# A third state of a selective scan is multiplied by C on TensorE, and the output copy keeps one buffer

## The chip, the cores and the metric

The kernel runs on one core of one Trainium2 chip. The time is device microseconds of one execution of the whole program, and a version's time is the median of its runs. The engines are named as the profile names them: PE is TensorE (its matmuls), PEld its weight loads, DVE is VectorE, ACT is ScalarE, POOL is GpSimd, and SP is SyncE, which here only issues DMAs.

## What is computed

The program is one layer of a metaformer on an input of 1024 channels and 64 x 64 pixels. A first part normalises and runs a decaying sum over channels. The second part is a bidirectional selective scan over the 4096 pixels as a sequence, and it takes most of the time:

```python
def step(h, inp):
    u_t, dt_t, B_t, C_t = inp
    dA = jnp.exp(dt_t[:, :, None] * A)
    h = dA * h + (dt_t * u_t)[:, :, None] * B_t[:, None, :]
    y = jnp.einsum('bdn,bn->bd', h, C_t)
    return (h, y)
...
y = (y_fwd + y_bwd) * jax.nn.silu(z.transpose(0, 2, 1))
out = y @ out_proj_w.T
```

There are 2048 inner channels d and 16 states n for each of them, and two directions. What the change touches is the second line of the recurrence's output: every state h[d, n, t] is multiplied by C[t, n] and the 16 products are summed.

## The kernel before

**Units.** `stage_scan` cuts the sequence into 8 chunks of T = 512 pixels and the inner channels into DB = 16 blocks of 128. One direction and chunk and block is a unit. There are 256: units 0 to 127 go backward, 128 to 255 forward. A chunk is 16 units in a row; below, the chunks are numbered 0 to 15. The code of each engine is written out unit by unit, and in a unit step by step for the states n = 0 to 15. Nothing reorders it: each engine runs its own list and waits on semaphores.

**One state on the engines.** In step n, ACT makes da = exp(delta * A[n]) into one of two PSUM banks (`da`, L1094), after it has saved the last column of the state of step n-2 (`save`, L1074); that save waits until scan n-2 is done. DVE runs the recurrence as one scan instruction (L1239), from `da`, the carried `state` and `w` = du * B, which POOL makes four states at a time (`weigh_b`, L1192). The result must then be multiplied by C and turned (pixels to partitions), and all 16 are summed in the PSUM bank `yT`. There are three ways for the product:

- states in VN (0, 1, 3, 6, 7, 9, 12 to 15): the scan writes PSUM (`h`), DVE multiplies by the broadcast C (`weigh`, L1249, into `hc`), and PE adds the transpose of `hc` into `yT` (L973, four 128x128 pieces);
- states in PN (2, 5, 8, 11): the scan writes SBUF (`hs`), POOL multiplies two states at once (`weigh_c`, L1202, into `hp`), and PE adds the transpose (L934);
- states in TN (4, 10): the scan writes SBUF, PE turns the state itself (`turn`, L868) into the bank `in_ps`, ACT copies it to `h_turned` (`turn_copy`, L1051), and PE multiplies it by a diagonal matrix of C (`add_turned`, L877) into `yT`. The diagonals `c_diag` are made by ACT (L1066) in the first unit of every chunk from the columns `c_col`, which SP loads as single elements (`load_c_columns`, L721).

DVE's multiplies don't stand behind each scan but in groups, behind the scans of 2, 5, 8, 11, 13 and 15.

**What else runs through the units.** PE works one chunk ahead: in backward units it projects x (`in_step`, L846, halves at steps 0 and 2, into `in_ps`), ACT copies it out at step 7 (L1025), PE runs the convolution as four diagonal matmuls into the bank `dt_ps` (`conv_step`, L853, step 5), and ACT copies that at step 10 (L1028). In forward units PE projects z for the unit itself, and the convolutions are for the chunk ahead. The last 16 backward units (chunk 7) project nothing and have an order of their own for the convolution (`TURN`: convolution at step 2, copy at 7). The bank `dt_ps` also takes the projection to dt (L841), which ACT reads at step 1 (`dt_read`, L994), in a chunk's last unit at step 4. ACT then makes `delta` for the next unit in the steps up to 6 (L999 to L1018).

**The output.** `yT_copy(b - 1)` (L1044) stands in ACT's step 2 of unit b and copies `yT` into one of two buffers `y_out`; SP stores it (L769). Ahead of the copy ACT waits for

```python
if b >= 1:
    act.wait_ge(S["stored"], stored_to(b - 1))
...
nc.scalar.activation(y_out[:, b % 2], yT[:], ACT.Copy).then_inc(S["yT_copied"], 1)
```

where `stored_to(b)` counts every store (yT, x, xc, z) that SP issues up to and with its unit b. SP waits in the same order: its unit b issues the stores of yT, xc and z, in a chunk's last unit also eight broadcasts of B and C (L713, 1 MB each) and the c columns between them, and at its end waits for `stored_to(b)` before it loads what the next units need.

## Time and profile before

| | |
|---|---|
| median of 3 runs | 8235.12 us (8234.53 to 8238.75) |
| the profiled execution | 8231.93 us, span 8230.1 us |
| the 256 units, from the first scan to the last | 728.4 to 7180.0 us |
| DVE busy, whole span | 7156.1 us (87%) |
| POOL busy | 6715.8 us (82%) |
| PE busy | 7136.7 us (87%) |
| ACT busy | 5349.8 us (65%) |
| granted TensorE clock, mean of the span | 0.959 |

The busy shares are of the whole span, with the stages ahead of and behind the scan. In a timeline the first column is the start in us from the span's start and the second the duration; instructions that follow one another are merged with their count. Two neighbours overlap by some 0.1 us at their ends, so what an instruction costs its engine is the distance to the next start, not its own duration. TensorE splits each float32 matmul of real data in two (8 in the trace for 4 in the code), and a transpose not. Steps below are given as "+x", in us after the start of the unit's first scan.

### The profile page before, as it was taken

What the parts mean: (1) busy time and instruction counts of PE and PEld (TensorE: products, weight loads), DVE (VectorE), ACT (ScalarE), POOL (GpSimd) and SP (SyncE); (2) the same over time, 40 slices, a digit from 0 to 9 for tenths busy, and PEclk for the clock granted to TensorE, in tenths of its full rate; (3) what the DMA queues carried; (4) which work ended last, traced back from release to release, by engine and by line L of the source; (5) the groups of instructions that cost most, each with busy time, mean ns of one, the idle gap of its engine ahead of it and who ended that gap; (6) DMA issues with size and microseconds to landing.
All of it is one profiled execution on the core that took longest, in us unless ns stands there. A gap on an engine that the chain in (4) does not pass through costs nothing. (4 is left out here: it accounts for less than half of the span.)

```text
span 8230.1 us, 114768 instructions
## 1 busy us (share of the span) xinstructions
PE 7136.7 (87%) x32512; PEld 4393.1 (53%) x32512; DVE 7156.1 (87%) x7788; ACT 5349.8 (65%) x12640; POOL 6715.8 (82%) x2320
## 2 busy tenths in 40 slices
PE   6578888888888888877899999999999988789999
PEld 3344555555555555554555555555555555534444
DVE  6913999999999999999999999999999999934443
ACT  6634777777777777777777777777777777610000
POOL 5513999999999999999999999999999999821110
PEclk8789999999999999998999999999999999889999
DMA  3363232323232323221323232323233332153442
GB/s 103 90 191 128 70 118 66 118 70 118 67 118 68 119 67 118 68 98 44 113 79 128 76 128 77 131 79 126 89 116 104 104 107 70 63 191 133 136 140 76
DMA packets 557719, 844.05 MB, mean 103 GB/s; under 512 B 129472, under 2 KB 276928, under 8 KB 539712
## 3 DMA queue, kind: packets, MB, share of 16 engines
q1 hardware_dynamic: 557120, 837.10, 31.1%
q8 instruction: 250, 4.10, 0.2%
q14 instruction: 349, 2.86, 0.1%
HBM read 583.89 MB, written 253.02 MB: 102 GB/s over the span
## 5 line engine op out<-in xcount | busy, mean ns | idle before, releaser
L1192 POOL TENSOR_TENSOR scan_w<-scan_du,scan_bcast_b 128x2048 f32<-128x2048 f32 x1023 | 4623.9, 4544 | 45.0 <-DVE scan_h L1239 6.6
L1239 DVE TENSOR_TENSOR_SCAN scan_h<-scan_da,scan_state,scan_w 128x512 f32<-128x512 f32 x2560 | 3185.3, 1276 | 44.2 <-ACT scan_da L1094 27.7
L1094 ACT ACTIVATE scan_da<-scan_delta,scan_prm 128x512 f32<-128x512 f32 x4096 | 2803.1, 685 | 0.0
L973 PE MATMUL scan_yT<-all_ident,scan_hc 128*128 128x128 f32 x10240 | 1540.1, 281 | 660.4 <-DVE scan_hc L1249 659.6
L1239 DVE TENSOR_TENSOR_SCAN scan_hs<-scan_da,scan_state,scan_w 128x512 f32<-128x512 f32 x1536 | 1891.9, 1258 | 45.2 <-ACT scan_da L1094 44.7
L973 PEld LDWEIGHTS scan_yT<-all_ident,scan_hc 128*128 128x128 f32 x10240 | 1175.3, 143 | 1395.5 <-DVE scan_hc L1249 1047.1
L846 PE MATMUL scan_in_ps<-scan_hn,scan_win 128*128 128x512 f32 x3840 | 1732.3, 594 | 13.6 <-issue 13.6
L1249 DVE TENSOR_TENSOR scan_hc<-scan_h,scan_bcast_c 128x512 f32<-128x512 f32 x2560 | 1637.3, 671 | 2.1 <-ACT scan_state L1074 0.7
L1202 POOL TENSOR_TENSOR scan_hp<-scan_hs,scan_bcast_c 128x1024 f32<-128x1024 f32 x512 | 1209.3, 2362 | 49.9 <-DVE scan_hs L1239 42.9
L846 PEld LDWEIGHTS scan_in_ps<-scan_hn,scan_win 128*128 128x128 f32 x3840 | 693.6, 191 | 715.6 <-issue 715.6
L1074 ACT ACTIVATE scan_state<-scan_h 128x1 f32<-128x1 f32 x2560 | 429.5, 168 | 982.8 <-DVE scan_h L1239 977.0
L853 PE MATMUL scan_dt_ps<-scan_x,scan_diag 128*128 128x512 f32 x1920 | 888.5, 606 | 101.2 <-ACT scan_x L1025 101.2
L1398 PE MATMUL out_o_ps<-out_yg,out_wout 128*128 128x512 f32 x2048 | 891.0, 594 | 0.0
L1366 POOL TENSOR_TENSOR out_yf<-out_yf,out_yb 128x512 f32<-128x512 f32 x128 | 162.5, 1270 | 744.7 <-DMA out_z<-z 744.7
L1398 PEld LDWEIGHTS out_o_ps<-out_yg,out_wout 128*128 128x128 f32 x2048 | 385.9, 191 | 464.8 <-issue 464.8
L1376 ACT ACTIVATE out_sz<-out_z 128x512 f32<-128x512 f32 x128 | 80.7, 630 | 826.1 <-DMA out_z<-z 826.1
L853 PEld LDWEIGHTS scan_dt_ps<-scan_x,scan_diag 128*128 128x128 f32 x1920 | 351.4, 193 | 480.9 <-issue 480.9
L877 PE MATMUL scan_yT<-scan_h_turned,scan_c_diag 128*128 128x128 f32 x4096 | 576.6, 287 | 0.0
L934 PE MATMUL scan_yT<-all_ident,scan_hp 128*128 128x128 f32 x4096 | 553.8, 280 | 0.0
L877 PEld LDWEIGHTS scan_yT<-scan_h_turned,scan_c_diag 128*128 128x128 f32 x4096 | 535.4, 204 | 0.5
L1427 DVE COPY out_o<-out_o_ps 128x512 f32<-128x512 f32 x64 | 44.2, 691 | 523.6 <-PE out_o_ps L1398 321.9
L934 PEld LDWEIGHTS scan_yT<-all_ident,scan_hp 128*128 128x128 f32 x4096 | 485.1, 146 | 0.0
(122 smaller groups left out, 6918.3 us busy)
## 6 DMA issues: line engine op xcount, KB each, us to landing
yT<-scan_y_out SPq DMA_DIRECT2D x257, 256.0 KB, 2.0
scan_win<-winx SPq DMA_DIRECT2D x128, 512.0 KB, 3.7
xc<-scan_xc_out SPq DMA_DIRECT2D x256, 256.0 KB, 2.0
scan_xc<-xc SPq DMA_DIRECT2D x256, 256.0 KB, 4.1
scan_bcast_b<-bc SPq DMA_DIRECT2D x64, 1024.0 KB, 8.0
scan_bcast_c<-bc SPq DMA_DIRECT2D x64, 1024.0 KB, 8.2
scan_win<-winz SPq DMA_DIRECT2D x128, 512.0 KB, 4.6
scan_x<-x_pad SPq DMA_DIRECT2D x128, 257.5 KB, 2.6
```

What stands on the lines that cost most here:

```text
L846: last = nc.tensor.matmul(bank, win[:, s, i], hn[:, i], start=(i == 0), stop=(i == KT - 1))
L853: last = nc.tensor.matmul(bank, diag[:, s, i], x[:, s, at:at + T], start=(i == 0), stop=(i == TAPS - 1))
L877: last = nc.tensor.matmul(yT[:, tb], c_diag[:, k, tb], h_turned[:, tb * P:(tb + 1) * P], start=False, stop=False)
L934: last = nc.tensor.matmul(yT[:, tb], hp[:, i, tb * P:(tb + 1) * P], ident[:], is_transpose=True, start=False, stop=False)
L973: last = nc.tensor.matmul(yT[:, tb], hc_slot(b, n)[:, tb * P:(tb + 1) * P], ident[:], is_transpose=True, start=(i == 0 and tb == 0), stop= ...
L1074: nc.scalar.activation(state_of(unit_, n_), h_slot(unit_, n_)[:, col:col + 1], ACT.Copy).then_inc(S["h_saved"], 1)
L1094: nc.scalar.activation(da[:, n % 2], delta[:, s], ACT.Exp, scale=decay(b, n)).then_inc(S["exp_done"], 1)
L1192: nc.gpsimd.tensor_tensor(w[:, g], du[:].unsqueeze(1).to_broadcast([P, G, T]), bcast_b[:, g * G:(g + 1) * G], ALU.mult).then_inc(S["w_done ...
L1202: nc.gpsimd.tensor_tensor(hp[:, i:i + 2], hs[:, HS[first]:HS[first] + 2], bcast_c[:, first:second + 1:second - first], ALU.mult).then_inc( ...
L1239: nc.vector.tensor_tensor_scan(flip(b, h_slot(b, n)), flip(b, da[:, n % 2]), flip(b, w[:, n // G, n % G]), state_of(b, n), ALU.mult, ALU.a ...
L1249: nc.vector.tensor_tensor(hc_slot(b, n), h_slot(b, n), bcast_c[:, n], ALU.mult).then_inc(S["hc_done"], 1)
L1398: last = nc.tensor.matmul(o_ps[:, q % 2], wout[:, q, b], yg[:, g, b], start=(b == 0), stop=(b == DB - 1))
```

## The change

State 1 moves from VN to TN. Its scan writes SBUF, DVE's multiply for it is gone, and PE turns it at step 3 into `dt_ps` (the other turned states still use `in_ps`), ACT copies it at step 7 ahead of the copy of the projection, and PE multiplies it by its diagonal at step 7. `y_out` has one buffer instead of two, so that `yT_copy` waits for the stores of one unit more. `TURN` goes, and chunk 7 uses `NORMAL`. The diagonals are 12 per chunk instead of 8, and start at step 2.

```diff
-TN = [4, 10]
+TN = [1, 4, 10]
...
-        y_out = sc.sb("y_out", [P, 2, TB, P])
+        y_out = sc.sb("y_out", [P, TB, P])
...
-        TURN = dict(diag=1, conv=2, xc=7, proj=8)
...
-            return [(a, TURN if back(b) and not back(a) else NORMAL)] if a < NU else []
+            return [(a, NORMAL)] if a < NU else []
...
-                return dict(mm=(6, 12), copy=(10, NS - 1), add=(12, NS - 1))
-            return dict(mm=(8, 12), copy=(12, NS - 1), add=(12, NS - 1))
+                return dict(mm=(3, 6, 12), copy=(5, 10, NS - 1), add=(5, 12, NS - 1))
+            return dict(mm=(3, 8, 12), copy=(7, 12, NS - 1), add=(7, 12, NS - 1))
+
+        def turn_bank(k):
+            return in_ps if k else dt_ps
...
-        C_DIAG_AT = (3, 3, 8, 8, 9, 9, 11, 11)
+        C_DIAG_AT = (2, 2, 3, 3, 8, 8, 9, 9, 11, 11, 13, 13)
...
                 pe.wait_ge(S["scan_done"], b * NS + TN[k] + 1 + SCR)
-                pe.wait_ge(S["in_copied"], (in_copies(b) if b or k else DB + 1) + 2)
+                if k == 0:
+                    pe.wait_ge(S["dt_read"], min(b + 2, NU))
+                    pe.wait_ge(S["xc_copied"], min(b + DB + 1, NU) + 2 if b else DB + 2)
+                else:
+                    pe.wait_ge(S["in_copied"], (in_copies(b) if b or k > 1 else DB + 1) + 2)
...
             def conv_step(a, b):
                 pe.wait_ge(S["dt_read"], min(b + 2, NU))
+                pe.wait_ge(S["h_turn_copied"], b * NTN + 1)
...
-                if b >= 1:
-                    act.wait_ge(S["stored"], stored_to(b - 1))
+                if b >= 0:
+                    act.wait_ge(S["stored"], stored_to(b))
                 act.wait_ge(S["hc_used"], (b + 1) * NV + NOUT)
-                nc.scalar.activation(y_out[:, b % 2], yT[:], ACT.Copy).then_inc(S["yT_copied"], 1)
+                nc.scalar.activation(y_out[:], yT[:], ACT.Copy).then_inc(S["yT_copied"], 1)
...
+                    if n == turn_steps(b)["copy"][0]:
+                        turn_copy(b, 0)
                     for i, when in in_steps_of(b):
                         if n == when["copy"]:
```

The lists of the engines show three places. The first is PE in an ordinary forward unit, from the first half of the projection on. Before (scan_hc is the product on its way into yT, scan_hs a state that is turned):

```order
L846 MATMUL scan_in_ps<-scan_hn,scan_win 128x512 x4
L973 MATMUL scan_yT<-all_ident,scan_hc 128x128 x8
L846 MATMUL scan_in_ps<-scan_hn,scan_win 128x512 x4
L973 MATMUL scan_yT<-all_ident,scan_hc 128x128 x4
L853 MATMUL scan_dt_ps<-scan_x,scan_diag 128x512 x4
L973 MATMUL scan_yT<-all_ident,scan_hc 128x128 x8
L934 MATMUL scan_yT<-all_ident,scan_hp 128x128 x8
L868 MATMUL scan_in_ps<-all_ident,scan_hs 128x128 x4
```

The same place in the changed kernel (its line numbers are 2 to 9 higher):

```order
L848 MATMUL scan_in_ps<-scan_hn,scan_win 128x512 x4
L980 MATMUL scan_yT<-all_ident,scan_hc 128x128 x4
L848 MATMUL scan_in_ps<-scan_hn,scan_win 128x512 x4
L874 MATMUL scan_dt_ps<-all_ident,scan_hs 128x128 x4
L980 MATMUL scan_yT<-all_ident,scan_hc 128x128 x4
L855 MATMUL scan_dt_ps<-scan_x,scan_diag 128x512 x4
L980 MATMUL scan_yT<-all_ident,scan_hc 128x128 x4
L883 MATMUL scan_yT<-scan_h_turned,scan_c_diag 128x128 x4
L980 MATMUL scan_yT<-all_ident,scan_hc 128x128 x4
L941 MATMUL scan_yT<-all_ident,scan_hp 128x128 x8
L874 MATMUL scan_in_ps<-all_ident,scan_hs 128x128 x4
```

Four transposes ahead of the projection's second half are gone, four stand behind it, and the product with the diagonal stands between the convolution and the next turn.

The second place is ACT in the first unit of a chunk, from its step 2 (scan_da is the exponential, scan_v a link of the chain to delta). Before:

```order
L1094 ACTIVATE scan_da<-scan_delta,scan_prm 128x512
L1044 ACTIVATE scan_y_out<-scan_yT 128x512
L999 ACTIVATE scan_v<-scan_v,scan_prm 128x512
L1074 ACTIVATE scan_state<-scan_h 128x1
L1094 ACTIVATE scan_da<-scan_delta,scan_prm 128x512
L1066 ACTIVATE scan_c_diag<-all_ident,scan_c_col 128x128 x2
L1074 ACTIVATE scan_state<-scan_hs 128x1
```

Changed:

```order
L1101 ACTIVATE scan_da<-scan_delta,scan_prm 128x512
L1073 ACTIVATE scan_c_diag<-all_ident,scan_c_col 128x128 x2
L1051 ACTIVATE scan_y_out<-scan_yT 128x512
L1006 ACTIVATE scan_v<-scan_v,scan_prm 128x512
L1081 ACTIVATE scan_state<-scan_hs 128x1
L1101 ACTIVATE scan_da<-scan_delta,scan_prm 128x512
L1073 ACTIVATE scan_c_diag<-all_ident,scan_c_col 128x128 x2
```

Two diagonals now stand ahead of the copy of yT. At step 7 of every unit the list gains one row ahead of the copy of the projection:

```order
L1101 ACTIVATE scan_da<-scan_delta,scan_prm 128x512
L1058 ACTIVATE scan_h_turned<-scan_dt_ps 128x512
L1032 ACTIVATE scan_z_out<-scan_in_ps 128x512
L1081 ACTIVATE scan_state<-scan_h 128x1
L1101 ACTIVATE scan_da<-scan_delta,scan_prm 128x512
```

The third place is SP in the last unit of a forward chunk, changed; before, the second c_col row had no x2, and nothing else differs:

```order
L715 DMA scan_bcast_c<-bc 128x2048 [waits scan_hc_done,scan_hp_done]
L723 DMA scan_c_col<-bc 128x4x1 [waits scan_c_diag_done]
L723 DMA scan_c_col<-bc 128x4x1 x2
L798 DMA z<-scan_z_out 128x512 [waits n1_transposed]
L691 DMA scan_x<-x_pad 128x515 [waits scan_stored,n1_var_ready]
```

A third column stands ahead of the store of z, and the load of x behind it is the first that waits for `stored`.

## Rows read from the trace of the kernel before

**Rows 1.** DVE's waits, 800 to 7000 us: total, times, longest.

```profile
DVE scan_hs L1239 <- ACT scan_da L1094: 39.2, 67, 1.2
```

**Rows 2.** DVE's timeline in a backward unit (it starts at 2404.32).

```profile
2403.14 1.26 DVE L1249 TENSOR_TENSOR scan_hc<-scan_h,scan_bcast_c 128x512 f32<-128x512 f32 x2
2404.32 2.45 DVE L1239 TENSOR_TENSOR_SCAN scan_h<-scan_da,scan_state,scan_w 128x512 f32<-128x512 f32 x2
...
2415.58 1.26 DVE L1239 TENSOR_TENSOR_SCAN scan_hs<-scan_da,scan_state,scan_w 128x512 f32<-128x512 f32 x1
...
2427.97 0.67 DVE L1249 TENSOR_TENSOR scan_hc<-scan_h,scan_bcast_c 128x512 f32<-128x512 f32 x1
```

**Rows 3.** POOL's timeline over the same unit.

```profile
2397.26 2.36 POOL L1202 TENSOR_TENSOR scan_hp<-scan_hs,scan_bcast_c 128x1024 f32<-128x1024 f32 x1
...
2422.11 2.35 POOL L1202 TENSOR_TENSOR scan_hp<-scan_hs,scan_bcast_c 128x1024 f32<-128x1024 f32 x1
```

**Rows 4.** ACT's timeline in the same unit, steps 5, 7 and 8.

```profile
2410.35 0.17 ACT L1074 ACTIVATE scan_state<-scan_h 128x1 f32<-128x1 f32 x1 [0.83 <-DVE scan_h L1239]
...
2414.28 0.58 ACT L1025 ACTIVATE scan_x<-scan_in_ps 128x512 f32<-128x512 f32 x1
2414.76 0.16 ACT L1074 ACTIVATE scan_state<-scan_h 128x1 f32<-128x1 f32 x1
2414.81 0.68 ACT L1094 ACTIVATE scan_da<-scan_delta,scan_prm 128x512 f32<-128x512 f32 x1
```

**Rows 5.** PE's timeline in a forward unit (it starts at 4444.94).

```profile
4450.61 3.60 PE L846 MATMUL scan_in_ps<-scan_hn,scan_win 128*128 128x512 f32 x8
4454.05 0.60 PE L973 MATMUL scan_yT<-all_ident,scan_hc 128*128 128x128 f32 x4
4454.48 3.60 PE L853 MATMUL scan_dt_ps<-scan_x,scan_diag 128*128 128x512 f32 x8
...
4462.81 0.66 PE L973 MATMUL scan_yT<-all_ident,scan_hc 128*128 128x128 f32 x4 [2.16 <-DVE scan_hc L1249]
4463.30 1.02 PE L858 MATMUL scan_proj_ps<-scan_xc_out,scan_wx 128*96 128x512 f32 x2
```

**Rows 6.** The unit at 4394.7, two units earlier, PE's timeline.

```profile
4412.55 0.67 PE L973 MATMUL scan_yT<-all_ident,scan_hc 128*128 128x128 f32 x4 [2.15 <-DVE scan_hc L1249]
4413.04 1.88 PE L858 MATMUL scan_proj_ps<-scan_xc_out,scan_wx 128*96 128x512 f32 x2
```

**Rows 7.** Windows: length, busy PE PEld DVE ACT POOL, clock, DMA share, GB/s.

```profile
3552.00:3967.00 415.00, 297.78 (x1536) 205.22 (x1535) 400.37 (x417) 299.24 (x745) 393.76 (x129) 0.89 0.20 65
4394.70:4419.60 24.90, 22.74 (x104) 14.01 (x103) 24.90 (x27) 18.76 (x47) 24.51 (x9) 0.93 0.25 79
4444.90:4469.80 24.90, 22.46 (x115) 14.13 (x113) 24.90 (x28) 19.20 (x49) 24.51 (x9) 1.00 0.24 80
```

**Rows 8.** Timeline of ACT and DVE in the unit at 4419.61, step 7 to 8.

```profile
4430.06 0.60 ACT L1025 ACTIVATE scan_z_out<-scan_in_ps 128x512 f32<-128x512 f32 x1 [0.43 <-PE scan_in_ps L846]
...
4431.34 1.28 DVE L1239 TENSOR_TENSOR_SCAN scan_hs<-scan_da,scan_state,scan_w 128x512 f32<-128x512 f32 x1 [0.38 <-ACT scan_da L1094]
```

**Rows 9.** SP's timeline at the end of a forward chunk.

```profile
4358.96 2.65 SPq L721 DMA_DIRECT2D scan_c_col<-bc  x2
4361.72 7.73 SPq L796 DMA_DIRECT2D z<-scan_z_out  x1
4374.77 0.33 SPq L689 DMA_DIRECT2D scan_x<-x_pad  x1
```

**Rows 10.** Line L721, the same two loads: from issue to landing.

```profile
DMA to landing us min/median/max: 12.7/13.6/14.6
```

**Rows 11.** ACT's timeline in the next chunk's first unit (it starts at 4369.02).

```profile
4371.61 0.60 ACT L1044 ACTIVATE scan_y_out<-scan_yT 128x512 f32<-128x512 f32 x1 [0.46 <-PE scan_yT L973]
...
4373.97 0.69 ACT L1066 ACTIVATE scan_c_diag<-all_ident,scan_c_col 128x128 f32<-128x128 f32 x2 [0.51 <-DMA scan_c_col<-bc]
```

**Rows 12.** DVE's timeline in a chunk's last unit (it starts at 4342.72), step 8.

```profile
4355.22 1.28 DVE L1239 TENSOR_TENSOR_SCAN scan_hs<-scan_da,scan_state,scan_w 128x512 f32<-128x512 f32 x1 [1.15 <-ACT scan_da L1094]
```

More of the change, by code:

```diff
@@ L769, in unit @@
                 sp.dma_start(yT_d[direction(b - 1)][(b - 1) % HALF + 1 if b else 0],
-                             y_out[:, (b + 1) % 2]).then_inc(S["stored"], LOAD)
+                             y_out[:]).then_inc(S["stored"], LOAD)
                 if at == DB - 1 and more:
@@ L830, in _ @@
             hold(sp, S["yT_copied"], NU + 1, S["passed"])
-            sp.dma_start(yT_d[0][HALF], y_out[:, 1]).then_inc(S["stored"], LOAD)
+            sp.dma_start(yT_d[0][HALF], y_out[:]).then_inc(S["stored"], LOAD)
             hold(sp, S["stored"], stored_to(NU - 1) + LOAD, S["passed"])
@@ L867, in turn @@
                 for tb in range(TB):
-                    last = nc.tensor.matmul(in_ps[:, tb * P:(tb + 1) * P], h_slot(b, TN[k])[:, tb * P:(tb + 1) * P],
+                    last = nc.tensor.matmul(turn_bank(k)[:, tb * P:(tb + 1) * P], h_slot(b, TN[k])[:, tb * P:(tb + 1) * P],
                                             ident[:], is_transpose=True, start=(tb == 0), stop=(tb == TB - 1))
@@ L903, in in_step @@
                     if b or i > DB:
-                        pe.wait_ge(S["h_turn_copied"], b * NTN if b else 1)
+                        pe.wait_ge(S["h_turn_copied"], b * NTN if b else 2)
                     in_proj(i % 2, 0, KT // 2)
@@ L1050, in turn_copy @@
                     act.wait_ge(S["h_turned_used"], b * NTN + k)
-                nc.scalar.activation(h_turned[:], in_ps[:], ACT.Copy).then_inc(S["h_turn_copied"], 1)
+                nc.scalar.activation(h_turned[:], turn_bank(k)[:], ACT.Copy).then_inc(S["h_turn_copied"], 1)
             def diagonal(s, db):
@@ L1136, in unit @@
                             xc_copy(a % 2, block_of(a))
-                    for k in range(NTN):
+                    for k in range(1, NTN):
                         if n == turn_steps(b)["copy"][k]:
```

## The prediction

> **What bounds the kernel now.** The page's busy shares come first: DVE and POOL are near full in every slice of the scan, PE is close, ACT is far from it. A share doesn't say which wait ends last, so the next view is DVE's waits: between 800 and 7000 us its largest wait is on ACT's exponential ahead of a scan into SBUF, 39.2 us over 67 times, the longest 1.2 [rows 1]. DVE is the bound, with some losses that ACT hands it. The third view is the timelines of one backward unit. The pair of multiplies ahead of the unit returns after 24.83 us [rows 2]; POOL's second pair product returns after 24.85 us [rows 3]. The reader is to see that both engines are full at the same pace. ACT then shows where it is tight: it starts step 5 as soon as scan 3 ends (it waited 0.83 for it), works without a pause, and its exponential of step 8 ends at 2415.49 for a scan that starts at 2415.58 [rows 2, 4]. There is no slack between the end of scan 3 and scan 8.
>
> **The ordinary unit.** Taken away: one DVE multiply. Two of them take from 2403.14 to 2404.32, so one costs 0.59 [rows 2]. It stood behind scan 2, ahead of scan 3, so scan 3 and ACT's step 5 come 0.59 earlier. Added in ACT's step 7: a copy of a PSUM bank, which costs what the copy there costs now, 0.48 to the next start [rows 4]. It lies in the very stretch that has no slack, so scan 8 comes 0.59 - 0.48 = 0.11 earlier, and with the 0.09 between exponential and scan used, 0.16 at best. Behind scan 8 nothing changes. A unit takes 24.72.
>
> Is the turned state there in time? PE loses four transposes ahead of the projection's second half and gains four behind it, 0.43 either way (4454.05 to 4454.48) [rows 5]. So it is ready when the projection was, at 4454.21 or +9.27. ACT asked for the projection at 2414.28, +9.96, and will now ask at +9.37 [rows 2, 4, 5]. The margin is 0.10; I count no wait. What is late next is the convolution, which now waits for that copy: it starts at about +10.0 instead of +9.54 [rows 5], and ends at +13.6. Queued behind it are the products of states 6 and 7; DVE has six buffers for them and doesn't notice. ACT copies the convolution in step 10, not before +14, so that is hidden. The product with the diagonal is 8 matmuls of the trace, 0.87 at the transposes' pace. PE waits 2.16 for the product of state 9 [rows 5]; 2.16 - 0.5 - 0.87 - 0.1 leaves 0.7, so PE has the room.
>
> POOL at 24.85 would be the next bound, but it runs ahead: at 2422.11, when it turns to the pair product, it has finished the four inputs for scans 0 to 3 of the next unit, which begins at 2404.32 + 24.83 = 2429.15 [rows 2, 3]: a lead of 7 us. A lag of 0.13 a unit uses up 1.8 us of that in the 14 ordinary units of a chunk, and the chunk's end gives it back. There are 15 x 14 = 210 ordinary units outside chunk 7: 210 x -0.11 = **-23.1 us**.
>
> **The clock in forward units.** In the forward chunks PE's work stands in one piece and its idle time too. After such a wait of 2.15 us the next two matmuls of the projection to B, C and dt take 1.88 us in one unit and 1.02 in another [rows 5, 6]; the granted clock is 0.93 over that unit and 1.00 over the other [rows 7], so for some microseconds it is the lower of its two levels, 1.2 GHz. The unit after it pays: the copy of z waits 0.43 for PE and scan 8 waits 0.38 [rows 8]. The units start at 4394.68, 4419.61 and 4444.94, so they take 24.93 and 25.33; against 24.83 the pair loses 0.6. It returns in every third unit, 0.2 a unit over the 98 ordinary units of chunks 8 to 14 (chunk 15 has no convolution). After the change the wait is split in two, 0.5 ahead of the convolution and 0.7 behind. I take it that the clock then stays at 2.4 GHz: 98 x -0.2 = **-19.6**. The other end is that the drops stay, and then every third unit also gets the 0.48 on top, since there ACT waits for PE: 0 instead of -19.6, and +0.16 x 98 = 16 more.
>
> The Trainium skill (TensorE: Matmul & The Clock Gate, What's actually happening) says that a throttled clock is the default and that activity releases it. By that rule more PE work in the gaps helps; rows 6 and 7 agree that the drop follows idle time. The sum above stands without it.
>
> **The first unit of a forward chunk.** This is the dear place. SP issues two c columns, then the store of z, whose issue alone takes 7.73 us, then waits for the stores until 4374.77 [rows 9], +5.7 of the next unit. The first column landed at 4358.96 + 12.7 = 4371.7 [rows 9, 10], the second when ACT's diagonal began, 4373.97 [rows 11]: a column costs 2.3. The third makes the columns land at +7.3 and the store behind them at about +8.0. Now ACT's copy of yT stands at +2.59 [rows 11] and waits for older stores only. In the changed kernel it stands behind two diagonals and waits for this store: +8.0. Behind it in ACT's queue is everything that leads to scan 8: copy, link and step 3 take 1.85 (4371.61 to 4373.97 - 0.51), two diagonals 0.6, step 4 two passes of some 0.65, steps 5 to 8 take 5.14 plus the new 0.48 [rows 4, 11], together 9.4. Scan 8 starts at +17.4. Today it is 2.59 + 1.85 + 0.51 + 0.6 + 1.3 + 5.14 = +12.0. That is 5.4 for each of 7 chunk starts (8 to 9 up to 14 to 15; the last has lighter work ahead of it, so one less): **+37**. Bounds: the column costs the store nothing, the copy starts at +5.7, 2.3 less, -16; or each of the three columns pushes the store once more, +16. In other units the same wait is free: a store takes about 2 us and the copy comes half a unit later.
>
> Again the page beside it: the Trainium skill (DMA: Bandwidth & Descriptors, Queues, rings and completion order) says that a DMA's increment lands only after every earlier write of the same DMA engine. By this rule z's completion must wait for the third column, as in my sum; without the rule the time would be 8228. Rows 9 and 10 fit: z was issued behind the second column and counted as landed 0.7 after it.
>
> **The other chunk edges.** A chunk's last unit reads dt late, and scan 8 waits 1.15 for ACT [rows 12], so the copy comes in full: 16 x 0.48 = **+7.7**. In the first unit of a backward chunk (and of chunk 8) the columns are early, there is no z, and ACT gets two diagonals ahead of the yT copy, 0.6, where it now waits 0.46 for PE as in [rows 11], plus 0.48: 8 x 0.6 = **+4.9**. Unit 0 waits for the columns too: **+2**.
>
> **Chunk 7.** 415 us for 16 units are 25.9 a unit, at a clock of 0.89 [rows 7]; DVE loses time because ACT waits in step 7 for the convolution. That copy moves to step 10, which frees step 7. But the convolution moves too, from +4 to +10. At 3.60 [rows 5] it ends at +13.6 and the unit is an ordinary one, -1.2. At the lower clock throughout it takes 7.2, ends at +17.2, and scan 11 (due at +15.4) comes 3.1 late, +1.9. PE idles more before it than today, so I take the middle, 0 for 15 units, with -18 and +28 as ends.
>
> **The sum.** -23.1 - 19.6 + 37 + 7.7 + 4.9 + 2 + 0 = +8.9. On the profiled execution's 8231.93 that is 8240.8; the median is 3.2 above it, so 8244.
>
> **The rivals.**
> - *The clock still drops in every third forward unit.* For it: the wait of 2.16 is followed by a drop in one unit and by none in another [rows 5, 6], so the length of that wait alone doesn't decide. Against it: the wait is what the change shortens, to a third. It decides if PE's longest wait stays near 2 us. 8244 + 19.6 + 16 = 8280, slower. Chance 0.15.
> - *The turned state is late.* ACT asks at +9.37 with a margin of 0.10; 0.2 of wait costs 42: 8286, slower. Chance 0.1.
> - *POOL binds.* If its lead is smaller than I think, units stay at 24.85 and the -23 is lost: 8267. Chance 0.06. Chunk 7 at its slow end gives 8272, chance 0.06.
> - *The store isn't pushed.* 8228, no change. Chance 0.13. With chunk 7 at its fast end too, 8210, faster; chance 0.17.
> - The forecast, gains and losses that cancel: chance 0.33.
>
> **How the numbers follow.** What is less than 0.2% (16.5 us) can't be told from no change here. Faster gathers the last case and some of the store's (0.2), slower the first four rivals less their near edge (0.35), the same holds the rest (0.45). The range leaves out the clock and the late turn at their far ends and what lies under 8210: 8208 to 8282.
>
> **What the next profile would show.** Right: DVE's scan 8 waits about 0.5 for ACT in every unit, the unit takes 24.7 in both directions, the granted clock of forward chunks is 1.00, PE's wait ahead of state 9's product falls to 0.7, and ACT's yT copy waits for a DMA once per forward chunk until +8. Wrong: a new wait of ACT on PE ahead of the turn's copy, a POOL product that DVE waits for, or a clock of 0.97 as before.

## The result and the profile after

The changed kernel takes 8221.5 us (median of 20 runs, 8212.26 to 8232.26), the kernel before 8232.15 in the same comparison (20 runs, 8217.56 to 8238.75). The ratio is 0.9987, 95% interval 0.9981 to 0.9993: a small gain, 10.7 us, where a loss of 8.9 us was forecast. Both values are within 0.2% of no change; the sign was forecast wrong.

The page of the profiled execution (8212.7 us, span 8210.9) has DVE at 7011.3 us (85%), PE at 7300.4 (89%), ACT at 5512.2 (67%), POOL at 6711.8 (82%). DVE does one multiply a unit less, PE and ACT do more. DVE's waits between 800 and 7000 us, total, times, longest (before: [rows 1]; there the scans into PSUM, scan_h, waited 6.4 us over 13 times):

```profile
DVE scan_hs L1248 <- ACT scan_da L1101: 136.7, 247, 3.0
DVE scan_h L1248 <- ACT scan_da L1101: 24.6, 22, 3.1
DVE scan_hs L1248 <- POOL scan_hp L1211: 5.0, 4, 2.2
```

DVE now waits for ACT in nearly every unit instead of in one of four, up to 3 us. In the lines of a timeline the square brackets give the engine's idle time ahead of the instruction and what ended it. The timelines of ACT and then of DVE in a backward unit (its scan 0 starts at 2389.90):

```profile
2399.26 0.58 ACT L1058 ACTIVATE scan_h_turned<-scan_dt_ps 128x512 f32<-128x512 f32 x1
2399.74 0.58 ACT L1032 ACTIVATE scan_x<-scan_in_ps 128x512 f32<-128x512 f32 x1
```
```profile
2400.99 1.28 DVE L1248 TENSOR_TENSOR_SCAN scan_hs<-scan_da,scan_state,scan_w 128x512 f32<-128x512 f32 x1 [0.34 <-ACT scan_da L1101]
```

The new copy stands in step 7, 0.48 from start to start, without a wait ahead of it: the turned state was there in time. That holds for all ordinary units; in the last units of 13 chunks ACT waits 1.13 us for PE's turn, where before it waited for PE's projection (0.59 in the unit at 4342.72). PE's timeline in a forward unit (its scan 0 starts at 4409.4), beside [rows 5]:

```profile
4418.09 0.60 PE L874 MATMUL scan_dt_ps<-all_ident,scan_hs 128*128 128x128 f32 x4
...
4419.47 3.67 PE L855 MATMUL scan_dt_ps<-scan_x,scan_diag 128*128 128x512 f32 x8 [0.34 <-issue]
...
4427.16 0.66 PE L980 MATMUL scan_yT<-all_ident,scan_hc 128*128 128x128 f32 x4 [0.94 <-DVE scan_hc L1258]
```

The wait of 2.16 has become 0.34 and 0.94. Windows over chunk 7, chunks 10 to 14 and chunk 15, columns as in [rows 7]:

```profile
3534.00:3959.00 425.00, 315.82 (x1667) 215.26 (x1666) 390.30 (x401) 310.01 (x767) 393.36 (x129) 0.82 0.20 65
4757.00:6763.00 2006.00, 1857.23 (x9592) 1208.43 (x9591) 1951.17 (x2001) 1597.10 (x3901) 1965.42 (x642) 1.00 0.32 104
6763.00:7163.00 400.00, 319.04 (x1750) 229.47 (x1749) 388.86 (x398) 284.18 (x691) 380.85 (x124) 0.95 0.17 58
```

The clock is 1.00 over whole forward chunks (0.97 before), but 0.82 in chunk 7, where it was 0.89, and chunk 7 is 10 us longer. Last, a forward chunk's first unit, whose scan 0 starts at 4356.64: SP's timeline, then ACT's, beside [rows 9, 11].

```profile
4346.85 9.22 SPq L723 DMA_DIRECT2D scan_c_col<-bc  x3
4356.18 0.46 SPq L798 DMA_DIRECT2D z<-scan_z_out  x1
```
```profile
4361.12 0.69 ACT L1073 ACTIVATE scan_c_diag<-all_ident,scan_c_col 128x128 f32<-128x128 f32 x2 [2.38 <-DMA scan_c_col<-bc]
4361.77 0.60 ACT L1051 ACTIVATE scan_y_out<-scan_yT 128x512 f32<-128x512 f32 x1
```

Issuing z now takes 0.46; the 7.7 us for which SP was held up fall on the third column. ACT waits for the columns to +4.5, then copies yT at +5.1. The forecast had +8.0.

**Where the time went.** The start of scan 0 of each unit in both traces gives the periods; their differences, after minus before, sum to the terms of the prediction (mean periods in brackets):

| term | forecast | measured, us |
|---|---|---|
| ordinary backward units, chunks 0 to 6 (97; 24.85 to 24.70) | -10.7 | -14.0 |
| ordinary units of chunks 8 to 14 (98; mean 25.05 to 24.70) | -30.4 | -33.9 |
| first units, forward chunks (7; 25.7 to 28.5; chunk 15 24.8 to 27.2) | +37 | +18.8 |
| first units, backward chunks and chunk 8 (7) | +4.2 | +2.3 |
| last units outside chunk 7 (14) | +6.7 | +7.1 |
| chunk 7 (415.3 to 424.9) | 0 | +9.6 |
| chunk 15 behind its first unit | -1.5 | +2.3 |
| units 0 and 1 | +2 | -1.9 |
| scan stage (the forecast has 1.6 more in chunk 7 and the very last unit) | +7.3 | -9.6 |

The two profiled executions differ by 19.2 us, the medians by 10.7. The scan stage's 9.6 is the change's; 7.0 of the rest lie ahead of the scans, in code that is the same: the first scan started anywhere between 721.3 and 734.4 us in the profiles of this study. So the experiments are read by the same decomposition, beside their ratio. Each is one profiled execution, and terms that an edit doesn't touch differ too: units 0 and 1 by up to 4.5 us in sum, the 14 last units by up to 4, chunk 7 by 1.

### The profile page after: what moved, and what is told of

It is laid out like the page before. It is cut to its first block and busy times, and to the rows that moved or that the text cites. A ratio compares the mean times of both kernels' runs of the same rounds, so it can differ in the third digit from the quotient of the medians.

```text
span 8210.9 us, 119471 instructions
## 1 busy us (share of the span) xinstructions
PE 7300.4 (89%) x34560; PEld 4560.6 (56%) x34560; DVE 7011.3 (85%) x7532; ACT 5512.2 (67%) x12960; POOL 6711.8 (82%) x2320
## 5 line engine op out<-in xcount | busy, mean ns | idle before, releaser
L1248 DVE TENSOR_TENSOR_SCAN scan_h<-scan_da,scan_state,scan_w 128x512 f32<-128x512 f32 x2304 | 2883.9, 1278 | 68.6 <-ACT scan_da L1101 52.3
L1248 DVE TENSOR_TENSOR_SCAN scan_hs<-scan_da,scan_state,scan_w 128x512 f32<-128x512 f32 x1792 | 2198.9, 1260 | 145.2 <-ACT scan_da L1101 140.1
L980 PE MATMUL scan_yT<-all_ident,scan_hc 128*128 128x128 f32 x9216 | 1443.9, 280 | 437.4 <-DVE scan_hc L1258 431.6
L980 PEld LDWEIGHTS scan_yT<-all_ident,scan_hc 128*128 128x128 f32 x9216 | 1066.0, 142 | 1016.6 <-DVE scan_hc L1258 678.4
L1258 DVE TENSOR_TENSOR scan_hc<-scan_h,scan_bcast_c 128x512 f32<-128x512 f32 x2304 | 1479.8, 669 | 0.5
L855 PE MATMUL scan_dt_ps<-scan_x,scan_diag 128*128 128x512 f32 x1920 | 926.6, 627 | 153.9 <-ACT scan_x L1032 101.1
L1081 ACT ACTIVATE scan_state<-scan_h 128x1 f32<-128x1 f32 x2304 | 386.9, 168 | 693.0 <-DVE scan_h L1248 692.3
L883 PE MATMUL scan_yT<-scan_h_turned,scan_c_diag 128*128 128x128 f32 x6144 | 819.2, 277 | 0.0
L883 PEld LDWEIGHTS scan_yT<-scan_h_turned,scan_c_diag 128*128 128x128 f32 x6144 | 753.2, 193 | 0.8 <-issue 0.5
L1081 ACT ACTIVATE scan_state<-scan_hs 128x1 f32<-128x1 f32 x1792 | 352.9, 197 | 237.1 <-DVE scan_hs L1248 236.0
```

Of the source, the lines that this page charges most:

```text
L855: last = nc.tensor.matmul(bank, diag[:, s, i], x[:, s, at:at + T], start=(i == 0), stop=(i == TAPS - 1))
L883: last = nc.tensor.matmul(yT[:, tb], c_diag[:, k, tb], h_turned[:, tb * P:(tb + 1) * P], start=False, stop=False)
L980: last = nc.tensor.matmul(yT[:, tb], hc_slot(b, n)[:, tb * P:(tb + 1) * P], ident[:], is_transpose=True, start=(i == 0 and tb == 0), stop= ...
L1081: nc.scalar.activation(state_of(unit_, n_), h_slot(unit_, n_)[:, col:col + 1], ACT.Copy).then_inc(S["h_saved"], 1)
L1248: nc.vector.tensor_tensor_scan(flip(b, h_slot(b, n)), flip(b, da[:, n % 2]), flip(b, w[:, n // G, n % G]), state_of(b, n), ALU.mult, ALU.a ...
L1258: nc.vector.tensor_tensor(hc_slot(b, n), h_slot(b, n), bcast_c[:, n], ALU.mult).then_inc(S["hc_done"], 1)
```

## The experiments

Ratios are to the kernel before in the same comparison, with the 95% interval. "Scan stage" is the sum of periods against that of the kernel before's profile, -9.6 for the change as given.

**The first unit of a forward chunk.** Three kernels take the two waits of ACT's copy apart.

```diff
-  act.wait_ge(S["stored"], stored_to(b))              # in yT_copy
+  act.wait_ge(S["y_stored"], (b + 1) * LOAD)          # own count; SP's yT store increments it
```

> The changed kernel, but ACT's copy of yT waits only for the store of yT before it, which gets a count of its own, and no longer for the store of z. The profile of the changed kernel has the copy at +5.1 us of the first unit of a forward chunk; the wait listed there is the diagonal's, ahead of the copy, for the c columns (gap 2.4 us, to +4.5), and z's store lands at +5.1. Theory A, the record's (the copy waits for z): the copy returns to +2.6, first forward units fall from 28.1 to about 25.7 us, 6 to 7 of them: 8205 us, ratio to before 0.997. Theory B (two waits end within 0.6 us, and the diagonals in front of the copy hold it alone): nothing moves, 8221 us, ratio 0.9987.

Measured: 8221.31, 0.9990 (0.9981 to 0.9999), scan stage -9.7. First forward units stay 2.7 us over before on average, as in the changed kernel. That is theory B's forecast.

```diff
-  C_DIAG_AT = (2, 2, 3, 3, 8, 8, 9, 9, 11, 11, 13, 13)
+  C_DIAG_AT = (3, 3, 4, 4, 8, 8, 9, 9, 11, 11, 13, 13)
```

> The changed kernel, but the diagonals of state 1 are built in ACT's steps 3 and 4 instead of 2 and 3, so behind the copy of yT. Theory C (the c columns alone hold the copy, the wait for z is empty): the copy returns to +2.6 and first forward units to about 25.7 us, 8205 us. Theory B (both waits end at about +5): the copy stays at +5.0, now for z's store, and the time stays within 3 us of 8221.

Measured: 8228.11, 0.9993 (0.9984 to 1.0002), scan stage -3.1. Now the same ACT copy names the other wait (timeline, unit at 4369.1):

```profile
4375.49 0.60 ACT L1051 ACTIVATE scan_y_out<-scan_yT 128x512 f32<-128x512 f32 x1 [4.26 <-DMA z<-scan_z_out]
```

So the wait is theory B's. The time isn't: it was to stay within 3 us of 8221, and the first forward units cost 26.0 us in sum instead of 18.8. Part of it is that two more diagonals (0.6 us) now come behind the wait instead of between the two; z also landed 0.3 us later on average in this profile.

> The changed kernel with both: the store of yT on a count of its own and the diagonals of state 1 in steps 3 and 4. All theories: the copy of yT at +2.6. Theory B expects that only this one of the three gains: first forward units 26.1 us (25.65 to 25.83 before, less 0.59 of multiply, plus 0.48 of copy and 0.6 of two more diagonals), so 2 to 3 us for each of 7: 8205 us, ratio 0.997. Theories A and C expect no more here than from the one part that each names.

Measured: 8208.06, 0.9971 (0.9962 to 0.9981), scan stage -20.6. The copy is at +2.0; first forward units cost 6.0 us in sum over before instead of 18.8. Taking away either wait alone gains nothing, taking away both gains 13 us. Two of these units still take 27.5 to 27.7 us, against 25.8 to 26.2 in the others. In them the columns' landing holds the diagonals in step 3 for 0.8 to 0.9, the granted clock is 0.94 instead of 1.00, and the convolution takes 5.37 us instead of 3.67, so that scan 11 waits 0.96 for ACT. PE's timeline in the unit at 4369.12:

```profile
4381.05 5.37 PE L856 MATMUL scan_dt_ps<-scan_x,scan_diag 128*128 128x512 f32 x8 [1.26 <-issue]
```

The changed kernel has two such units (29.4 and 29.1 us, clock 0.94), so a part of its +18.8 comes by way of a longer convolution and not directly of a wait for a DMA.

**What a column costs.** Two parts of the change are put alone into the kernel before.

```diff
-  c_col = sc.sb("c_col", [P, NTN, TB])
+  c_col = sc.sb("c_col", [P, NTN + 1, TB])     # and a load of state 1's column behind the two
```

> The kernel before, with one edit: SP also loads the c column of state 1, which nobody uses (the diagonals wait for all three). The record's step: a column costs 2.3 us of DMA time at a chunk's start, so the last one lands at +7.3 of a forward chunk's first unit (+4.95 before) and the diagonals start then: 2.3 us for each of 8 chunk starts, 8247. Theory from the profile of after (all that was issued by then lands when the broadcasts' backlog is through, and the third column only takes over the 7.6 us for which SP was held up in the store of z): the last column lands at +4.5 to +5, z at +5 to +5.7, and the time stays at 8230.

Measured: 8231.04, 0.9999 (0.9989 to 1.0009), scan stage -0.4. In chunk starts 9 to 14 the last column lands at +5.2 to +5.7 and z at +5.8 to +6.4 (before 4.9 to 5.1 and 5.6 to 5.8). So the third column costs 0.4 us there, not 2.3. At the start of chunk 9 the three columns land at +2.7, +3.0 and +5.3: the second, which landed at +4.9 before, is early now, and the third is late in its place. The last 1 MB broadcast lands between these two, at +4.7. SP's timeline shows the hold-up on the column here too:

```profile
4348.40 10.24 SPq L722 DMA_DIRECT2D scan_c_col<-bc  x3
4358.75 0.84 SPq L797 DMA_DIRECT2D z<-scan_z_out  x1
```

> The kernel before, with the single buffer for y alone (copy waits for all stores of the unit before). In before z lands at +5.7 and ACT's copy of yT stands at +2.6, with the diagonals behind it. If the wait for z is a cost by itself, first forward units rise by 3 us, 7 x 3 = 21: 8250. If nothing in the queue behind it is urgent, 8230.

Measured: 8244.95, 1.0017 (1.0008 to 1.0027), scan stage +17.9, of it +20.0 in the first units of the seven forward chunks. ACT's waits between 4360 and 6800 us have

```profile
ACT scan_y_out L1044 <- DMA z<-scan_z_out: 22.7, 6, 4.3
```

The buffer alone is a loss of 14 us by the medians.

In the last unit of a chunk z was then issued in two other places, in the kernel with the diagonals in steps 3 and 4:

```diff
 # z_store_first
     broadcast(chunk + 1, 1, 1)
+    z_d store
     load_c_columns(chunk + 1)
-    z_d store
 # before_the_broadcast
+    z_d store
+    load_c_columns(chunk + 1)
     store_xc(a)
     broadcast(chunk + 1, 1, 1)
-    load_c_columns(chunk + 1)
-    z_d store
```

> The changed kernel with the diagonals of state 1 in steps 3 and 4 (8228 by itself) and one more edit: in a chunk's last unit SP issues the store of z ahead of the c columns, not behind them. Theory (what is issued before SP's 7.6 us hold-up lands early, as the first column does at +2.0; what is issued behind it lands at +5): z lands by +2.2, ACT's copy stands at +2.0 to +2.3, and the time is that of the version with an own count, 8208. Rival (z lands late wherever it is issued): 8228.

Measured: 8225.22, 0.9993 (0.9983 to 1.0003), scan stage -4.6. The theory of the hold-up fell: z was issued at -9.8 us and landed at +5.8 all the same (+3.7 to +6.8 over the seven chunk starts). The timelines of SP and ACT:

```profile
4350.83 0.32 SPq L715 DMA_DIRECT2D scan_bcast_c<-bc  x1
4351.26 0.37 SPq L797 DMA_DIRECT2D z<-scan_z_out  x1
4351.74 5.20 SPq L723 DMA_DIRECT2D scan_c_col<-bc  x3
...
4366.85 0.60 ACT L1053 ACTIVATE scan_y_out<-scan_yT 128x512 f32<-128x512 f32 x1 [3.70 <-DMA z<-scan_z_out]
```

The broadcast of C ahead of it, 1024 KB, took 15.3 us from issue to landing, to 4366.2; z landed 0.65 behind it. That is how the changed kernel reads too: this broadcast was issued at 4346.42 and landed 14.1 us later, at 4360.5, the last column at 4361.1, z at 4361.7. At all seven starts of forward chunks z lands 1.0 to 1.1 us behind this broadcast in the kernel before, 1.0 to 1.2 in the changed one and 0.6 to 0.7 here, wherever SP was held up. Hence the last run.

> The changed kernel with the diagonals of state 1 in steps 3 and 4 (8228 by itself); in the last unit of a chunk SP issues the store of z and the three columns ahead of the last 1 MB broadcast of C and the store of xc, not behind them (in the other forward units z goes ahead of xc too). In the profile of the changed kernel that broadcast lands at 4360.53, the last column at 4361.09, z at 4361.74; with z issued right behind the broadcast and ahead of the columns it landed 0.65 after the broadcast again. Theory (z lands late because the broadcast is ahead of it in the queue, whatever the columns do): z and the columns land by +2.6, ACT's copy of yT stands at +2.0 to +2.6 in the first units of forward chunks, and the time is that of the own count, 8208. Rival (what is stored or loaded at that time lands at +5 in any place of the queue): 8225.

Measured: 8211.82, 0.9973 (0.9962 to 0.9983), scan stage -20.9. Timelines of SP and ACT (scan 0 at 4366.3):

```profile
4353.81 0.37 SPq L793 DMA_DIRECT2D z<-scan_z_out  x1
4354.28 9.46 SPq L723 DMA_DIRECT2D scan_c_col<-bc  x3
...
4369.29 0.60 ACT L1052 ACTIVATE scan_y_out<-scan_yT 128x512 f32<-128x512 f32 x1 [0.84 <-DMA xc<-scan_xc_out]
```

z lands at +0.4, and the copy starts at +2.9, held only by the store of xc that now stands behind the columns; first forward units cost 7.4 us in sum instead of 26.0. So z landed late because of what SP had issued ahead of it, of which the last broadcast is 1 MB and xc 256 KB. It isn't a strict order, though: at six of the seven chunk starts z now landed 0.3 to 0.6 us ahead of a 1 MB broadcast of B that was issued ahead of it (at 4353.33 here, landed at 4367.4). Why z passes this one and not the last broadcast of C wasn't tested.

**Chunk 7.** There the change had replaced the steps of the convolution (2, its copy 7, the product with wx 8) by the ordinary ones (5, 10, 11).

```diff
+  TURN = dict(diag=1, conv=2, xc=7, proj=8)      # chunk 7 and unit 111; turned in in_ps there
-  return [(a, NORMAL)] if a < NU else []
+  return [(a, TURN if back(b) and not back(a) else NORMAL)] if a < NU else []
```

> The changed kernel, but in the 17 units whose next input is a forward one and which project nothing (unit 111 and chunk 7) the convolution is back in step 2, its copy in step 7 and the product with wx in step 8; state 1 is turned in the projection's bank, which is free there. Theory (the convolution, delayed to +10 and run at the lower clock, ends so late that scan 11 waits): chunk 7 falls from 424.9 us to about 414 (415.3 before), 8210 us, ratio to before 0.9974. Rival (chunk 7 is slow because PE's clock is low over its longer idle time, wherever the convolution stands): it stays above 420.

Measured: 8234.45, 1.0001 (0.9992 to 1.0010), chunk 7 at 437.5 us. Neither forecast: slower than the changed kernel, not to be told from the kernel before, and a chunk 7 that is slower than in both. The timelines of PE, ACT and DVE in the unit at 3709.67:

```profile
3714.83 4.82 PE L859 MATMUL scan_dt_ps<-scan_x,scan_diag 128*128 128x512 f32 x8
3719.49 0.60 PE L878 MATMUL scan_in_ps<-all_ident,scan_hs 128*128 128x128 f32 x4
```
```profile
3720.12 0.60 ACT L1063 ACTIVATE scan_h_turned<-scan_in_ps 128x512 f32<-128x512 f32 x1 [1.03 <-PE scan_in_ps L878]
3720.62 0.68 ACT L1040 ACTIVATE scan_xc_out<-scan_dt_ps,scan_convp 128x512 f32<-128x512 f32 x1
```
```profile
3721.97 1.28 DVE L1253 TENSOR_TENSOR_SCAN scan_hs<-scan_da,scan_state,scan_w 128x512 f32<-128x512 f32 x1 [1.56 <-ACT scan_da L1106]
```

The transposes of state 1 stand behind a convolution of 4.8 us in PE's queue (3.67 in a forward unit at the full clock), and two copies stand ahead of scan 8. Scan 13 waits another 1.28 for ACT, and a unit takes 27.3. So the place that the change gave the convolution is better than the old one for three turned states. In the changed kernel itself the convolution is late for scan 11. Timelines of PE, ACT and DVE there, unit at 3588.55:

```profile
3598.59 5.08 PE L855 MATMUL scan_dt_ps<-scan_x,scan_diag 128*128 128x512 f32 x8 [0.54 <-issue]
```
```profile
3603.77 0.69 ACT L1035 ACTIVATE scan_xc_out<-scan_dt_ps,scan_convp 128x512 f32<-128x512 f32 x1 [2.49 <-PE scan_dt_ps L855]
```
```profile
3605.14 1.28 DVE L1248 TENSOR_TENSOR_SCAN scan_hs<-scan_da,scan_state,scan_w 128x512 f32<-128x512 f32 x1 [1.12 <-ACT scan_da L1101]
```

The convolution starts at +10.0 in every unit of chunk 7 but the first (+10.9), ends between +15.1 and +16.7 as the clock lets it (0.87 or 0.81 over the unit), ACT stands in step 10 for it and scan 11 waits. Where it ends at +15.1 the unit takes 25.5, where it ends at +16.7, 27.05 or more: a microsecond of it is one of the unit. The next kernel puts it between: turned in the free bank, conv=4, xc=10, proj=11, with the own count and the diagonals in steps 3 and 4.

> The version with own count for yT's store and diagonals in steps 3 and 4, and in unit 111 and chunk 7 state 1 turned in the projection's bank while the convolution stands in step 4 of PE's queue, copied in ACT's step 10. In the run with the convolution in step 2 and its copy in step 7, ACT waited 1.0 us for PE's turn in step 7, then had two copies there, and scan 8 came 1.6 late. Theory (in chunk 7 it is the place of the two copies and of the convolution that costs): the convolution ends by +13 even at the lower clock, units take 24.7 to 25.3, chunk 7 falls from 424.9 us to 395 to 405: 8208 - 22 = 8186 us, ratio 0.9945. Rival (the low clock alone costs, by way of state 4's turn for scan 13): units 25.5 or more, 8200.

Measured: 8177.91, 0.9938 (0.9924 to 0.9951), scan stage -48.4; chunk 7 takes 400.8 us. The convolution stands behind another wait of PE and so starts at +9.3, not earlier, and ends at +13.9 to +15.5, later than I expected. Where it ends by +14 the unit takes 24.3 to 24.4, at +14.5 24.8 and at +15.4 25.8, which continues the relation of the changed kernel. The low clock alone doesn't make chunk 7 slow: at 0.86 a unit takes 24.3 if the convolution ends by +14. The windows of this kernel's chunk 7:

```profile
3542.80:3943.60 400.80, 304.62 (x1666) 215.51 (x1665) 389.67 (x402) 310.53 (x767) 394.71 (x130) 0.84 0.21 71
```

The clock is 0.84, against 0.82 where it took 424.9. Chunk 7 gives 24 of the 28 us by which this scan stage is shorter than that of own_count_diag_3. This kernel is 0.5% faster than the changed one and the fastest here.

**PE's clock.** Two kernels shorten the wait of [rows 5] in the kernel before; one delays the convolution in forward units, the other adds eight transposes.

```diff
 # before_conv_later, conv_step
+  if not back(b):
+      pe.wait_ge(S["scan_done"], b * NS + 6 + 1 + SCR)
 # before_more_transposes, turn
-  for tb in range(TB):
+  for tb in list(range(TB)) * (3 if k == 0 and b and not back(b) else 1):
```

> The kernel before, with one edit: in forward units PE starts the convolution only after scan 6 has ended (about +10.0 us instead of +9.5). ACT, DVE and the number of matmuls stay. PE's one wait of 2.16 us becomes two, about 0.5 and 1.6. Theory (what took the clock's drops away is that the wait is split): granted clock 1.00 in chunks 9 to 14, forward units 24.84, 98 x -0.2 = -20 us, 8212. Rival (the changed kernel's eight more matmuls a unit and their shorter waits did it): clock 0.97 and the three periods 24.84, 24.93, 25.33 as before, 8232.

Measured: 8213.44, 0.9978 (0.9968 to 0.9988); the 98 forward units give -20.1, the clock over chunks 9 to 14 is 1.00. PE's timeline:

```profile
4434.74 3.67 PE L853 MATMUL scan_dt_ps<-scan_x,scan_diag 128*128 128x512 f32 x8 [0.51 <-issue]
...
4442.39 0.66 PE L975 MATMUL scan_yT<-all_ident,scan_hc 128*128 128x128 f32 x4 [1.79 <-DVE scan_hc L1251]
```

> The kernel before, with one edit: in forward units PE does the four transposes of state 4's turn three times (the same result into the same bank), 0.87 us more work directly ahead of its wait for state 9's product. The wait falls from 2.16 to about 1.3 us and stays in one piece. Theory of the rival (more work, shorter idle): clock 1.00 and forward units 24.84, 8212. Theory of the split alone: the drops stay, 8232. Slower than 8240 if the turned state then comes late to ACT.

Measured: 8220.13, 0.9986 (0.9977 to 0.9995); the 98 units give -20.6 at a clock of 1.00, and chunk 15, whose units have no convolution, loses 9.5 behind its first unit. PE's timeline:

```profile
4432.84 1.47 PE L868 MATMUL scan_in_ps<-all_ident,scan_hs 128*128 128x128 f32 x12
4435.59 0.66 PE L973 MATMUL scan_yT<-all_ident,scan_hc 128*128 128x128 f32 x4 [1.28 <-DVE scan_hc L1249]
```

Both ways work, a wait split in 0.5 and 1.8 and a wait of 1.3 in one piece, so "the split alone" is wrong: what the two have in common is that the longest wait is shorter than 2.16. The sum of PE's idle time isn't what they share: 2.6 us a unit in the first, 1.6 in the second, 2.2 to 2.4 in the kernel before. The backward units of the kernel before agree, with 2.6 us of idle time, a longest wait of 1.33 and a clock of 1.00. Eight useless transposes gain 0.14%. In chunk 15 three of four units have a clock of 0.87 to 0.93, and scan 13 waits 0.3 to 1.7 us for ACT in them; why wasn't tested.

**What would bind next.**

```diff
+  if k == 0 and b:
+      act.sem_inc(S["h_turn_copied"], 1)      # in turn_copy, in place of the copy
+      return
```

> The changed kernel, without ACT's copy of the turned state 1 in every unit but the first (0.48 us of ACT in step 7; TensorE multiplies what h_turned held before, so y is not the reference's). It asks what the next bound is. By the account of the record scan 8 comes 0.48 earlier, and a unit would take 24.22. POOL is busy 24.4 us a unit, so if POOL binds next the unit stops between 24.4 and 24.6. 240 units x -0.1 to -0.48: 8105 to 8197 us; I expect the POOL case, 24.5 and 8175.

Measured: 8181.21, 0.9944 (0.9928 to 0.9959). Outside chunks 0, 7 and 15, units take 24.35 for the first 4 to 8 of a chunk, then about 24.85 (24.80 to 24.90). POOL's timeline in one of those (scan 0 at 1843.98):

```profile
1856.60 2.36 POOL L1214 TENSOR_TENSOR scan_hp<-scan_hs,scan_bcast_c 128x1024 f32<-128x1024 f32 x1
1859.04 0.61 POOL L1189 TENSOR_SCALAR scan_u<-scan_xc 128x512 f32<-128x512 f32 x1
1859.74 1.28 POOL L1192 TENSOR_TENSOR scan_du<-scan_delta,scan_u 128x512 f32<-128x512 f32 x1
1861.15 4.55 POOL L1204 TENSOR_TENSOR scan_w<-scan_du,scan_bcast_b 128x2048 f32<-128x2048 f32 x1
1865.65 2.36 POOL L1214 TENSOR_TENSOR scan_hp<-scan_hs,scan_bcast_c 128x1024 f32<-128x1024 f32 x1
1867.95 13.58 POOL L1204 TENSOR_TENSOR scan_w<-scan_du,scan_bcast_b 128x2048 f32<-128x2048 f32 x3
```

No gaps over 0.14: POOL needs 24.86 a unit, more than the 24.70 that DVE takes after the change. DVE lives on POOL's lead, which is built up at a chunk's edge. In chunk 3 POOL has the inputs for scans 0 to 3 ready 6.9 us ahead of the unit at first; this falls by 0.5 a unit to 3.2, and there the units go from 24.35 to 24.86. In the changed kernel the lead falls by about 0.2 a unit, from 7.5 to 5.0 over the chunk, and lasts. What binds then is POOL's product, by way of PE, whose timeline reads ahead of the unit at 1843.98:

```profile
1843.18 1.09 PE L941 MATMUL scan_yT<-all_ident,scan_hp 128*128 128x128 f32 x8 [0.81 <-POOL scan_hp L1214]
```

In a unit of 24.35, at 1645.84, PE doesn't wait there. PE is then late with the turn (+9.2 instead of +8.7), ACT waits 0.58 for it and scan 8 0.54 for ACT. My expectation of 24.4 to 24.6, from POOL's busy time, was wrong; the pace of a queue without gaps is read from start to start.

## Why the prediction was wrong, step by step

- **Ordinary unit, right.** 24.70 against 24.72; the new copy comes out of the gain in the stretch up to scan 8 (the prediction's "0.16 at best" is a slip, 0.11 and 0.09 are 0.20; the sum doesn't use it), and DVE's wait of 0.34 there is the one foretold as about 0.5 (start to start of scans 7 and 8 grew from 1.2 to 1.64).
- **Turned state in time, right** for the ordinary units. The wait of ACT on PE that was named as a sign of being wrong exists, but only in units 0, 1 and 255 and in the last units of 13 chunks, 1.13 us each, where ACT had waited for PE before too.
- **Clock in forward units, right**, -20 of the -34 us; the two kernels above show it alone. The Trainium skill (TensorE: Matmul & The Clock Gate, What's actually happening) has activity release the throttled clock; before_more_transposes agrees, with its 8 extra transposes and the clock at 1.00, but before_conv_later reaches 1.00 with no more work than the kernel before.
- **The first unit of a forward chunk: the step that failed.** The prediction says "a column costs 2.3. The third makes the columns land at +7.3 and the store behind them at about +8.0." I took the distance of two landings for the cost of a transfer. A third column cost 0.4 in the kernel before, and in the changed kernel the columns landed at +4.5 and z at +5.1. Between the two columns of the kernel before (4371.6 and 4373.95) the 1 MB broadcast landed, at 4373.6, and z follows it. The bound that I gave for this, "the column costs the store nothing, the copy starts at +5.7", is close to what happened, and the term is +18.8 instead of +37. These 18.2 us turn the sign: the forecast stood 18.5 above the scan stage's -9.6, and the other misses cancel. The bound was listed only as a rival of 0.13 and 0.17. The single buffer itself does cost, as forecast: alone, it makes the copy wait for z and costs 20 us in these units.
- **The copy's wait, half right.** It was said to wait for z. It has two waits that end within 0.7 us, z's and the columns' by way of the diagonals ahead of it; each covers the other.
- **Chunk 7, mis-sized**: +9.6 against 0. The slow end of the range had the mechanism (the convolution at the lower clock, scan 11 late by 3.1; it waits 2.7 in the unit at 3561.5, and 3.0 at most); taking the middle between it and the fast end was not founded on a row.
- **Last units and first backward units**: +7.1 and +2.3 against 6.7 and 4.2. Chunk 15 was wrong by 3.8: its units now take 24.70, 25.25 and 25.13 in turn, at clocks of 1.00, 0.93 and 0.93; in the last two scan 13 waits 0.3 to 0.4 for ACT, and ACT before it 1.1 to 1.3 for PE's turn of state 4. What starts the cycle wasn't tested.
- The Trainium skill (DMA: Bandwidth & Descriptors, Queues, rings and completion order) has a completion wait for earlier writes of the same DMA engine. It gives no time, and the time is where my sum went wrong. z's landing fits it in the kernel before, the changed one and z_store_first (0.65 us behind the broadcast at 4366.18). In before_the_broadcast z landed ahead of a broadcast issued before it, and in the changed kernel two columns issued behind the broadcast landed 1.5 and 1.8 us ahead of it. No run shows which DMA engines each transfer used, so the rule is neither confirmed nor refuted here.

## What to carry to other kernels

When two transfers land 2.3 us apart, look what else landed between them before calling that the price of one: here a 256 KB store landed right behind the 1 MB broadcast that was issued ahead of it, wherever SP was held up, and moving it ahead of that broadcast brought it 5 us forward. If a copy drains an output bank, look whether it waits for its own store or for a count that other stores share. Two waits that end together must be taken away together; one alone reads as "no effect". A shorter longest wait of TensorE can be worth more than the work that is saved: here 20 of 34 us in the forward units.

## What the runs showed of the hardware

- SP was held up for about 7.7 us in one DMA at each of these places, whichever it was: z in the kernel before (7.73), the third column in the changed one (9.22 for three). Columns and z together took 10.4 us of issuing before, 9.7 after and 11.1 with the third column alone (at the start of chunk 9), so the long issue isn't the cost of the DMA that shows it. Nor does it set the landing: at the start of chunk 12 in the kernel before z took 0.43 us to issue, and landed at +5.7 as elsewhere.
- A store of 256 KB issued 9.8 us ahead of a unit landed at +5.8 (z_store_first), one issued at -0.5 at +5.1 (the changed kernel): in this queue an earlier issue behind the same broadcast bought nothing. Of two or three 2 KB columns issued behind the broadcast, all but the last landed ahead of it, the last behind it.
- With a longest wait of PE of 2.16 us a unit the clock fell in every third forward unit, with 1.79 or 1.28 it stayed at 1.00 over chunks 9 to 14; in chunk 7, with two waits of 2.7 to 3.0 a unit, it was 0.89 in the kernel before and 0.82 in the changed one.
